# The state products of an mLSTM kernel behind the first part of a down projection

## The reference

```python
x = x + xattn(layernorm(x), ctx, ctx, gates, norm_w)   # 8 heads of 64
x = x + ffn(layernorm(x), w_gate, w_up, w_down)        # 512 -> 1408 -> 512
# xattn, of each head:
log_D = log_f_cum[s] - log_f_cum[t] + ig[t]            # t <= s, else -inf
D = exp(log_D - max_t log_D)
C = (q @ k.T) / 8 * D
h = C / (max(|sum_t C|, exp(-max_log_D)) + 1e-6) @ v   # then a norm of each head
# ffn: activations and weights are rounded to FP4 in blocks of 16
h = silu(q4(x) @ q4(w_gate).T) * (q4(x) @ q4(w_up).T)
y = q4(h) @ q4(w_down).T
```

## Time and profile before

| | |
|---|---|
| median of 3 runs | 1877.68 us (1873.64 to 1881.2) |
| the profiled execution | 1876.42 us, of which the span of the instructions is 1874.7 us |
| PE matmul | 93% busy |
| PE weight load | 51% |
| DVE | 84% |
| ACT | 73% |
| POOL | 63% |
| DMA | mean 113 GB/s |
| granted PE clock, mean | 0.972 |

### The profile page before, as it was taken

One profiled execution on the slowest core, in us unless ns is written; L12 is line 12 of the kernel. 1 busy time (PEld: TensorE's weight loads), 2 busy tenths in 40 slices (PEclk: granted clock), 3 DMA queues, 4 the chain that ended last, 5 costly groups with the idle time before them and its releaser, 6 DMA issues. The chain is left out here.

```text
span 1874.7 us, 41843 instructions
## 1 busy us (share of the span) xinstructions
PE 1737.2 (93%) x14073; PEld 950.2 (51%) x14073; DVE 1571.9 (84%) x3341; ACT 1366.4 (73%) x2815; POOL 1182.1 (63%) x1188
## 2 busy tenths in 40 slices
PE   3545999999999999999999999999999999999997
PEld 2423555555555555555555555555555555555543
DVE  8985888888888888889888888888797888889994
ACT  7764777777777777777777777777787777776663
POOL 7854666667566756666666665656666675656652
PEclk9666999999999999999999999999999999999998
DMA  6342444445444544444454544434444454444332
GB/s 216 102 91 68 117 108 117 126 117 123 106 122 116 122 111 115 125 112 118 111 127 107 122 118 117 115 102 122 116 117 112 117 133 101 117 105 106 93 67 64
DMA packets 342134, 211.77 MB, mean 113 GB/s; under 512 B 275200, under 2 KB 281856, under 8 KB 341920
## 3 DMA queue, kind: packets, MB, share of 16 engines
q1 hardware_dynamic: 341920, 209.10, 43.9%
HBM read 125.93 MB, written 17.30 MB: 76 GB/s over the span
## 5 line engine op out<-in xcount | busy, mean ns | idle before, releaser
L482 PE MATMUL bank<-wgTh,xqT 128*128 128x512 f16 (+1 forms) x1536 | 556.6, 362 | 25.4 <-DMA xqT<-xqs 25.4
L482 PE MATMUL bank<-wuTh,xqT 128*128 128x512 f16 (+1 forms) x1536 | 556.2, 362 | 0.0
L1059 POOL TENSOR_TENSOR stage<-stage,hs 128x512 f32<-128x512 f32 (+1 forms) x192 | 190.5, 992 | 409.8 <-DVE stage L1267 409.8
L609 PE MATMUL bank<-wdTh,work 128*128 128x512 f16 x704 | 268.9, 382 | 12.9 <-DMA work<-stage 12.8
L482 PE MATMUL bank<-wgTl,xqT 128*128 128x512 f16 (+1 forms) x768 | 278.4, 363 | 0.0
L482 PE MATMUL bank<-wuTl,xqT 128*128 128x512 f16 (+1 forms) x768 | 278.2, 362 | 0.0
L610 PE MATMUL bank<-wdTl,work 128*128 128x512 f16 x704 | 267.5, 380 | 0.0
L611 PE MATMUL bank<-wdTh,work 128*128 128x512 f16 x704 | 267.3, 380 | 0.0
L482 PEld LDWEIGHTS bank<-wgTh,xqT 128*128 128x128 f16 x1536 | 150.6, 98 | 186.4 <-DMA xqT<-xqs 33.1
L1112 POOL TENSOR_TENSOR stage<-stage,hinv 128x512 f32<-128x512 f32 (+1 forms) x192 | 234.1, 1221 | 8.1 <-DVE hinv L1352 8.1
L482 PEld LDWEIGHTS bank<-wuTh,xqT 128*128 128x128 f16 x1536 | 150.6, 98 | 147.3 <-issue 1.2
(11 more groups left out here) (206 smaller groups left out, 3725.4 us busy)
## 6 DMA issues: line engine op xcount, KB each, us to landing
mb<-max_dram SPq DMA_DIRECT2D x64, 512.0 KB, 4.2
x<-in_x_dram SPq DMA_DIRECT2D x64, 256.0 KB, 2.9
cf<-in_ctx_dram SPq DMA_DIRECT2D x64, 256.0 KB, 3.7
cn<-in_ctx_dram SPq DMA_DIRECT2D x64, 256.0 KB, 3.8
wb<-warp_dram SPq DMA_DIRECT2D x128, 128.0 KB, 3.0
out_dram<-ob SPq DMA_DIRECT2D x64, 256.0 KB, 3.7
xb<-in_x_dram SPq DMA_DIRECT2D x60, 256.0 KB, 2.7
work<-stage SPq DMA_TRANSPOSE x192, 3.1
```

The costliest lines, as they stand in the source:

```text
L482: i = e.matmul(o[:, 0:width], x, w[:, c, n0:n0 + width], start=first and k < 2, stop=last and k >= 4)
L609: e.matmul(DOWN[:, :], hi, wdT[0][:, c0 + c, :], start=(c0 + c == 0), stop=False)
L1059: e.tensor_tensor(blocks(hx[:, n0:n0 + w]), blocks(hx[:, n0:n0 + w]), per_block(hs2[:, n0 // BLOCK:(n0 + w) // BLOCK]), ALU.mult).then_inc ...
```

## The change

`pe_st_mm(t6)` is moved in `pe_turn` from right behind `pe_u(t6)` to behind `pe_down(t9, 0)`. Nothing else is changed: the same instructions, the same waits in front of each, the same start-up list.

```diff
@@ -657,9 +657,10 @@
                 pe_gu(e, t8, 2)
             if t6.live(NT):
                 pe_u(e, t6)
+            if t9.live(NT):
+                pe_down(e, t9, 0)
+            if t6.live(NT):
                 pe_st_mm(e, t6)
-            if t9.live(NT):
-                pe_down(e, t9, 0)
             if t9.live(NT):
                 pe_down(e, t9, 1)
             if t1.live(NT):
```

More of the change, by code:

```diff
@@ L659, in pe_turn @@
                 pe_u(e, t6)
-                pe_st_mm(e, t6)
             if t9.live(NT):
                 pe_down(e, t9, 0)
+            if t6.live(NT):
+                pe_st_mm(e, t6)
             if t9.live(NT):
```

## The result

The changed kernel takes 1885.87 us in the median of 6 runs (1882.75 to 1887.73), against 1877.41 us before in 6 runs of the same series. The ratio is 1.0046, with a 95% interval of 1.003 to 1.0063: 8.5 us slower. The forecast was +3.8 us, 1881.5 us, with a range of 1874 to 1889. The profiled execution takes 1887.73 us, 1.9 us over its median, and its span is 11.3 us longer than that of before. Of this, 1.7 us lie ahead of the first turn, where the list of the start-up is the same in both, 7.5 in the turns, and 2.0 behind the last of them. What the first and the last part come from was not tested.

The account below looks back on a forecast made before the run. The prediction took PE's own stream as the bound. Tiling steps +6.9, late turns +0.1 and freed xqT waits -3.2 gave +3.8 us on 1876.42, 1880.2; with the median 1.26 higher, 1881.5 us, range 1874 to 1889.

Parts of the forecast that it names:

- PE's stream is the bound, and nothing waits at the old place: PE waits only about 25 us in 1479 us, never in front of line 592's products, so no stall to remove.
- Ways out and in, 0.10 and 0.09 us: PE leaving 128x64 tiles behind the D block costs 0.10 us; re-entering them from down matmuls to products costs 0.09.
- The sum of the neighbours: Both extra tiling steps on PE together cost 0.197 us a turn; over 35 ordinary turns, +6.9 us.
- The cover of St: Products end 2.79 us later; DVE's St has 3.70 us of cover in the tightest ordinary turn, so stays put.
- The gate turns absorb it: In 14 turns with gate work, the 0.2 us disappears in PE's 1.09 us wait for St before the scores: 0.
- the collisions spread: Rival: 13 more turns wait for xqT and none slides out, +16.5 us, 1894 us; chance 0.08.
- Five of seven stretched turns slide out: Five of seven turns waiting for xqT ahead of gate turns lose that wait, 0.64 us each: -3.2 us.
- 9 or so: Sign in the changed kernel's profile: the list of PE's waits for xqT has 9 or so in place of 14.
- The packet follows PE's place in its list, while the transpose follows DVE: In the seven turns, the instruction packet comes 0.197 us later against the transpose of xqs, past stretching it in five.
- The stretched turns absorb the move: In seven turns ahead of gate turns, PE waits for xqT at its end; added cost at first sight 0.
- the collisions stay: Rival: all seven turns still wait for xqT, +7.0 us, 1884.7 us; chance 0.3.

Follow-up runs that it names:

- e1: Kernel before with the state products on the whole array, in the old place, odd heads using their neighbour's vk: 1886.02 us, ratio 1.0046.
- e2: Kernel before with the same whole-array products (odd heads using their neighbour's vk) behind the first down piece: 1882.83 us, ratio 1.0032.
- e3: Changed kernel with the products, on their 128x64 tiles, behind the second down piece, ahead of the scores: 1936.33 us, ratio 1.0314.
- e4: Changed kernel with its products in two halves, one in the middle of the first down piece, one behind it: 1886.06 us, ratio 1.0045.

## Why the prediction was right, and where it was off

- *PE's stream is the bound, and nothing waits at the old place*: right. PE's printed waits are smaller after the change, and the time is larger.
- *Ways out and in, 0.10 and 0.09 us*: right to the hundredth, in the changed kernel, and shown by e1 and e2 to be the tiling. The Trainium skill ("TensorEngine Tiling (Array Packing)", "Tiling Modes") says that a change of tiling mode drains TensorE. The runs agree, with 0.31 us from a down matmul into 128x64 products and 0.22 us into products on the whole array.
- *The sum of the neighbours*: mis-sized. The term "0.197 us a turn" measured 0.256. I had taken the products' own time as unchanged. Behind a change of tiling the block of sixteen takes 0.62 us in place of 0.57. The warm-up held this too: the block there, behind a down matmul, takes 0.69 us by the timeline's duration, against 0.64 in an ordinary turn. With 0.01 us more in the down rows, this is 2 us on 35 turns.
- *The cover of St*: right, also in size. DVE has no wait for line 592, and in the tightest turn 0.86 us is left where 0.91 was worked out; in e3, 2.6 us later, it is gone. The cover of the gate turns, 5.5 us by the earlier trace rows, is one and a half times the 3.70 and not twice.
- *The gate turns absorb it*: right. Their wait for St fell from 1.10 to 0.84 us, and the length of those that aren't stretched stayed 29.42 us. That two more are stretched, +1.5 us, was the rival "the collisions spread" at a small scale, and not in the forecast.
- *Five of seven stretched turns slide out*: wrong, and the largest error, 3.2 us. None slid out. Stretched transposes rose from 14 to 17 in the steady turns. The sign "9 or so" waits for xqT seemed to come true, with 10, but by luck: seven of the eight stretched ordinary turns end in no wait now, or in one so short (0.11 us at most) that the list leaves it out. And a turn freed of its stretch would have gained less than was reckoned, since a stretched ordinary turn was 0.74 us longer than a plain one, and not 0.84. The step that failed is "The packet follows PE's place in its list, while the transpose follows DVE". In the changed kernel the packet of instructions again moves 2.6 to 2.9 us after the transpose's issue. The issue is at 1005.49; the time to landing of that transpose in the DMA view, and the window from 1008.1 to 1008.3 us in it:

```profile
xqT<-xqs SPq DMA_TRANSPOSE x1, 4.8
```

```profile
q8 instruction: 1, 0.02, 29.2%
```

  By PE's place it should have come later: PE's scores, the block ahead of it, started at 1007.09 here and at 998.72 before, so the packet came 1.1 us behind their start, and 1.8 us before the change. In all profiles the packet of a stretched transpose starts 2.57 to 2.91 us after the issue, however the orders differ.

  The trace of before could have told that this packet doesn't follow PE's place. The seven stretched ordinary turns there are four turns apart, and from one to the next each packet falls a little later in the turn by its place in the list. The packet that is one earlier in the list moves with this: it starts 7.23, 7.62, 8.45, 8.80, 8.93, 9.34 and 9.93 us after the turn's first gate matmul. The one in the transpose doesn't: 24.46, 24.40, 24.47, 24.41, 24.45, 24.24 and 24.31 us. In the changed kernel it is the same, 6.6 to 9.9 us for the one and 24.0 to 24.2 for the other in eight turns, and there the transpose too is issued 0.3 us earlier in the turn. So the packet's start goes with the transpose. Why is open: it may be held back until then. Open is also whether the packet stretches the transpose, or both are late by a third cause. The offset isn't enough to tell a stretched one: at 307.4 us in the changed kernel a packet comes at 2.62 us, and the transpose takes 3.1 us.
- *The stretched turns absorb the move*: right. They went from 26.48 to 26.19 us, even shorter than before. The DVE chain up to the transpose ends 0.3 us earlier against PE's turn: in the median the issue is 21.34 us after the first gate matmul, and was 21.64. What changed there are the two operations behind `dve_out` at the begin of DVE's turn. The timeline of DVE in such a turn, of before and of the changed kernel:

```profile
976.23 0.75 DVE L1244 SCALAR_TENSOR_TENSOR ob<-bank,osc,x 128x512 f32<-128x512 f32 x1 [1.86 <-PE bank L611]
976.89 0.76 DVE L1256 SCALAR_TENSOR_TENSOR x<-un,x 128x512 f32<-128x512 f32 x1
...
977.59 1.53 DVE L1262 SCALAR_TENSOR_TENSOR stage<-work,stage 128x512 f32<-128x512 bf16 x1
```

```profile
984.35 0.75 DVE L1245 SCALAR_TENSOR_TENSOR ob<-bank,osc,x 128x512 f32<-128x512 f32 x1 [2.48 <-PE bank L611]
985.01 1.18 DVE L1257 SCALAR_TENSOR_TENSOR x<-un,x 128x512 f32<-128x512 f32 x1
...
986.12 0.68 DVE L1263 SCALAR_TENSOR_TENSOR stage<-work,stage 128x512 f32<-128x512 bf16 x1
```

  From the start of the first to the end of the third it is 2.89 us before and 2.45 after; 0.1 us of this is lost again ahead of the transpose. Operations of the same shape take 0.7 to 1.5 us there, and the long ones run beside one step of POOL (line 1112, 1113 in the changed kernel): it lasts from 977.08 to 978.57 us beside the 1.53 us before, and from 984.59 to 985.65 beside the 1.18 us after, while the operation of 0.68 us has it no more. That this is the reason was not tested.

The rival nearest to the measured time was "the collisions stay", +7.0 us by the old price. With 0.256 in place of 0.197 it would have said +9, and +8.5 was measured. That this is so near is in part luck: in the profiled executions the turns give +7.5 us, in which +1.5 in newly stretched gate turns and -2.0 in the stretched ordinary ones nearly cancel. The sum of the forecast, +3.8, was short by more than half.

## What to carry to other kernels

On a PE-bound stretch, count the changes of tiling: keep products of one tiling together, and take the price of a detour from block to block, including the block itself. A move of a few tenths of a us for each turn is as small as what the kernel gains or loses by some idle instructions ahead of its list, so compare variants with more than one shift of the list before believing a difference under 0.5%. Stalls that absorb a cost hide its size: read PE's stream and its waits apart, as in e4, where the price doubled and the time stood still.

## What was not expected of the hardware

- A DMA transpose of 3.1 us takes 4.7 to 5.1 us in some turns, and in each of them a 16 KB packet of PE's instructions starts 2.57 to 2.91 us after its issue. The reverse doesn't hold: in several turns with such a packet the transpose takes 3.0 to 3.4 us. With gate work in the turn a stretch costs 0.90 us. 64 to 192 idle instructions ahead of PE's list changed the number of stretched gate turns from 7 to 0, 0, 0 and 2. They made the kernel before 0.3 to 0.4% faster, which beats both kernels of this case, but in part by an earlier start of the turns.
- Sixteen products of 65 columns in f32 on 128x64 tiles take 0.57 us behind others of their tiling, and 0.62 us behind a change of it.
